# A perceiver layer on one core: the last unit's down products and scatter in column halves, three gathers ahead of a low part on GpSimd

## The chip, the cores and the metric

The kernel runs on one core of one Trainium2 chip. The metric is the time of one execution in microseconds, measured on the device. Smaller is better. The core has five engines with instruction streams of their own: TensorE (PE in the profile; PEld is its loading of stationary operands), VectorE (DVE), ScalarE (ACT), GpSimd (POOL) and SyncE (SP), and sixteen DMA engines that they share. Engines wait for each other through semaphores.

## The reference

One layer of a perceiver: a cross attention of 512 tokens over 8192 context rows, a causal self attention, and a feed-forward part of experts. Everything is float32. The change lies in the last part:

```python
x_flat = x.reshape(Bx * Tx, H)                      # 512 x 512
scores = jax.nn.softmax(x_flat @ gate_w.T, axis=-1)
_, topk_ids = jax.lax.top_k(scores, 2)              # 2 of 8 experts for a token
w = scores * in_topk
gu = jnp.einsum('nh,eih->nei', x_flat, experts_gate_up)
g, u = (gu[..., :704], gu[..., 704:])
h = jax.nn.silu(g) * u
expert_out = jnp.einsum('nei,ehi->neh', h, experts_down)
out = jnp.einsum('neh,ne->nh', expert_out, w)
out = out + shared_weight * shared                  # an expert that sees all tokens
return x + out
```

## The kernel before

**Splitting.** Each float32 operand of a product is split in two: a high part (a rounded copy, made by ScalarE) and a low part (the rest, made by VectorE or GpSimd as `raw - high`). A product is the sum of three: high x high, high x low, low x high. Names end in `_hi` and `_lo`.

**Units.** After the shared expert, the kernel goes through units. A unit is one expert and up to 128 of the token rows routed to it. Each of the eight experts has one unit; experts with more rows have a further one. With these inputs three are added, so units 0 to 10 run, and `final` is 10. The rows of all units lie in a DRAM tensor, `slots`, 128 rows per unit; a unit's result goes back to the place its rows came from. A unit has three hidden chunks (`CH`), of 256, 256 and 192 columns. `up(u, c)` computes both sides of a chunk (12 matmuls), `turn_hidden(u, c)` transposes the product of silu and side, and `down(u, c)` adds the chunk's part to the unit's 128x512 output in bank 2 of PSUM (6, 6 and 5 matmuls).

**The order on TensorE** is written by hand in `unit` (lines 1314 to 1342). The third down part of a unit is done inside the next one: `up(u, 0)`, `down(u - 1, 2)`, `up(u, 1)` and so on. `down(u, 2)` waits for `dn_last_ready >= u + 1`, that is, for the low part of the unit's third down weights, `wd_lo[2]`. For units 0 to 9 GpSimd makes it (`down_last_low`, line 533, waiting for the high part and for the first low part of the next unit's sides); for unit 10 VectorE does. SyncE's load of the next unit's third down part into `raw_d[2]` waits for the same semaphore (line 375).

**What happens to a unit's output.** Units 0 to 8: ScalarE copies it to `y_out` (`keep`), SyncE stores it to `slots` (line 392), nine stores, each adding 16 to `y_stored`. Units 9 and 10 are not stored. Their output is weighed and split (`output_high` on ScalarE, `output_low` on VectorE), and TensorE adds it to the token order by a product with `back`, a 0/1 matrix: `scatter(0)` for unit 9, `scatter(1)` for unit 10, each four token tiles of high and four of low part, into banks 4 to 7. All other tokens' results are gathered: GpSimd issues eight indirect DMAs (`gather_kept`, line 538), four token tiles for each of the two experts of a token (`c`), from `slots` to `met`. Ahead of them stands a wait for all nine stores and an add of one column (line 547). Three semaphores tell of them: `met_full` (four of c=0), `met_second` (c=1, tiles 0 and 1), `met_rest` (c=1, tiles 2 and 3).

**The tail.** VectorE adds six of the eight gathered tiles to `x` with their weight (`add_met`, line 1907). For c=1, tiles 2 and 3, ScalarE multiplies by the weight (line 860) and GpSimd adds (line 554). At last VectorE adds the four banks of the scatter (line 1988), the fourth in two column halves, and each of these adds releases a store: 256 KB for the first three tiles, 128 KB for each half of the fourth, from SyncE (lines 422, 424) and ScalarE (862, 864). Between the last down product and `scatter(1)` TensorE runs warming matmuls (`keep_warm`, line 901).

```python
pool.wait_ge(y_stored, (final - 1) * 16)
pool.tensor_tensor(blank[:, 0:1], blank[:, 0:1], blank[:, 1:2], ALU.add)
gather_kept(0, 0, ST, met_full)
gather_kept(1, 0, 2, met_second)
gather_kept(1, 2, ST, met_rest)
```

## Time and profile before

| | us |
|---|---|
| median of 3 runs | 697.93 (696.33 to 698.01) |
| the profiled execution | 697.82 |
| its span, first to last instruction | 696.1 |
| TensorE busy | 687.5 (99%) |
| VectorE busy | 554.6 (80%) |
| ScalarE busy | 339.2 (49%) |
| GpSimd busy | 211.2 (30%) |
| mean granted clock of TensorE | 0.998 |

The span is the time from the first to the last instruction that the profiler recorded in one execution; the execution's own time is 1.7 us longer. Busy times are sums over the span: they say that TensorE hardly rests, and not which engine is late in the last 30 us, where the change lies. A row of a timeline gives the start, the duration, the engine, the source line, the operation and its tiles; in brackets the idle time before it and what ended it. Matmuls are pipelined: a row's duration is its way through the engine, and the distance of two starts is what it costs. The releaser is inferred from semaphore events.

### The profile page before, as it was taken

The numbers are of one execution on the slowest core, as the hardware profiler recorded it, in microseconds if no ns is written. First come the engines' busy times: TensorE is split into PE (matmuls) and PEld (weight loads), VectorE is DVE, ScalarE is ACT, GpSimd is POOL, SyncE is SP. The second block draws the span as 40 slices with busy tenths as digits, with TensorE's granted clock in tenths as the row PEclk, the third lists the DMA queues.
The fourth block names the chain that finished last, engine by engine and source line by source line (L and its number), as shares of the span: only waits on it lengthen the run. The fifth ranks groups of instructions, "written<-read, shape, count | busy, mean of one in ns | idle before, by whom it ended". The sixth has DMA issues, their size and how long they took to land.

```text
span 696.1 us, 9883 instructions
## 1 busy us (share of the span) xinstructions
PE 687.5 (99%) x3195; PEld 568.7 (82%) x3195; DVE 554.6 (80%) x730; ACT 339.2 (49%) x454; POOL 211.2 (30%) x156
## 2 busy tenths in 40 slices
PE   8999999999999999999999999999999999999997
PEld 7788888888888788888888888888888888878875
DVE  5688877777989998899996853779435799999997
ACT  4422222222245565556663334642234588888872
POOL 5954545545430000000000001236884111211245
PEclk9999999999999999999999999999999999999999
DMA  8057677777742236432210602514200899999984
GB/s 305 15 171 220 214 226 238 245 219 239 246 139 92 91 121 282 152 110 90 90 60 0 252 37 81 234 72 144 91 1 6 312 345 386 370 392 374 378 320 151
DMA packets 38974, 130.70 MB, mean 188 GB/s; under 512 B 6690, under 2 KB 10788, under 8 KB 35876
## 3 DMA queue, kind: packets, MB, share of 16 engines
q1 hardware_dynamic: 36548, 124.72, 50.8%
q0 software_dynamic: 1536, 4.20, 1.9%
q10 hardware_dynamic: 864, 1.44, 0.6%
q8 instruction: 14, 0.23, 0.1%
q14 instruction: 12, 0.10, 0.1%
HBM read 120.89 MB, written 9.46 MB: 187 GB/s over the span
## 4 chain that ended last, share of the span: by engine, by line
PE 80%; DVE 6%; DMA 6%; issue 3%; ACT 3%; SPq 1%; DVEq 0%
PE ps L1065 25%; PE ps L1005 8%; PE ps L1006 8%; PE ps L1009 8%; DMA raw_u<-up_in 5%; PE ps L891 4%; PE ps L893 4%; PE ps L892 4%; PE ps L1258 4%; ACT wu_hi L749 2%; DVE wu_lo L1849 2%; PE ps L958 2%; DVE wd_lo L1855 2%; PE ps L1192 1%; DMA wk<-wk_in 1%
## 5 line engine op out<-in xcount | busy, mean ns | idle before, releaser
L468 POOL TENSOR_TENSOR c_lo<-ring,c_hi 128x512 fp32r<-128x512 f32 x64 | 87.7, 1371 | 86.4 <-ACT c_hi L615 86.4
L615 ACT ACTIVATE c_hi<-ring 128x512 fp32r<-128x512 f32 x64 | 40.4, 634 | 126.4 <-PE ps L1009 82.9
L485 POOL TENSOR_TENSOR w_lo<-raw,w_hi 128x1024 fp32r<-128x1024 f32 x11 | 26.5, 2408 | 247.4 <-ACT w_hi L736 234.6
L1005 PE MATMUL ps<-qk_hi,c_hi 128*128 128x512 f32 x256 | 99.8, 390 | 0.0
L1006 PE MATMUL ps<-qk_lo,c_hi 128*128 128x512 f32 x256 | 99.6, 389 | 0.0
L1494 DVE TENSOR_TENSOR runmax<-runmax,att 128x512 f32<-128x512 f32 x64 | 83.9, 1311 | 3.9
L1488 DVE SCALAR_TENSOR_TENSOR att<-ring,beta,ps 128x512 f32 (+1 forms) x64 | 47.7, 746 | 26.6 <-PE ps L1009 25.7
L1009 PE MATMUL ps<-qk_hi,c_lo 128*128 128x512 f32 x256 | 68.6, 389 | 0.0
L1065 PE MATMUL ps<-p_hi,d_hi 128*128 128x512 f32 x256 | 63.8, 391 | 0.0
L1065 PE MATMUL ps<-p_hi,d_lo 128*128 128x512 f32 x256 | 63.2, 389 | 0.0
L1065 PE MATMUL ps<-p_lo,d_hi 128*128 128x512 f32 x256 | 63.2, 389 | 0.0
L749 ACT ACTIVATE wu_hi<-raw_u 128x2048 fp32r<-128x2048 f32 (+1 forms) x33 | 58.7, 1778 | 6.0 <-DMA raw_u<-up_in 5.8
L1849 DVE TENSOR_TENSOR wu_lo<-raw_u,wu_hi 128x1024 fp32r<-128x1024 f32 x40 | 51.8, 1294 | 11.4 <-ACT wu_hi L749 11.1
L533 POOL TENSOR_TENSOR wd_lo<-raw_d,wd_hi 128x1024 fp32r<-128x1024 f32 x10 | 24.1, 2413 | 117.7 <-DVE wu_lo L1849 117.7
L639 ACT ACTIVATE d_hi<-ring 128x1024 fp32r<-128x1024 f32 x32 | 33.9, 1059 | 50.0 <-PE ps L1065 49.3
L1005 PEld LDWEIGHTS ps<-qk_hi,c_hi 128*128 128x128 f32 x256 | 48.0, 188 | 10.5 <-DVE qk_lo L1468 0.6
L1065 PEld LDWEIGHTS ps<-p_lo,d_hi 128*128 128x128 f32 x256 | 48.1, 188 | 10.0
L1065 PEld LDWEIGHTS ps<-p_hi,d_lo 128*128 128x128 f32 x256 | 48.1, 188 | 10.0
L1009 PEld LDWEIGHTS ps<-qk_hi,c_lo 128*128 128x128 f32 x256 | 48.0, 188 | 10.0
L1065 PEld LDWEIGHTS ps<-p_hi,d_hi 128*128 128x128 f32 x256 | 47.6, 188 | 10.5 <-DVE ps L1590 0.8
L1006 PEld LDWEIGHTS ps<-qk_lo,c_hi 128*128 128x128 f32 x256 | 48.1, 188 | 9.9
L1267 PE MATMUL ps<-wu_hi,xg_hi 128*128 128x512 f32 (+1 forms) x132 | 50.9, 386 | 0.0
(340 smaller groups left out, 1507.1 us busy)
## 6 DMA issues: line engine op xcount, KB each, us to landing
ring<-stream SPq DMA_DIRECT2D x64, 512.0 KB, 4.3
raw_u<-up_in SPq DMA_DIRECT2D x22, 1024.0 KB, 7.0
raw_d<-down_in SPq DMA_DIRECT2D x33, 512.0 KB, 7.9
ring<-ctx_in SPq DMA_DIRECT2D x32, 512.0 KB, 3.3
raw<-shared_in SPq DMA_DIRECT2D x11, 768.0 KB, 6.1
raw_u<-up_last_in SPq DMA_DIRECT2D x11, 768.0 KB, 7.5
slots<-blank SPq DMA_DIRECT2D x15, 256.0 KB
late<-wqkv_in SPq DMA_DIRECT2D x1, 3072.0 KB, 10.3
```

Source lines behind the costliest of these rows:

```text
L468: pool.tensor_tensor(c_lo[:, s % 2, :], ring1[:, s, 0, :], c_hi[:, s % 2, :].bitcast(F32), ALU.subtract).then_inc(lo1_ready, 1)
L615: act.activation(c_hi[:, s % 2, :], ring1[:, s, 0, :], ACT.Copy).then_inc(hi1_ready, 1)
L639: act.activation(d_hi[s % 2][:, :, :], ring2[:, s, :, :], ACT.Copy).then_inc(hi2_ready, 1)
L749: act.activation(wu_hi[c][:, :, :], raw_u[c][:, :, :], ACT.Copy).then_inc(up_hi_ready, 1)
L1005: pe.matmul(ps[:, s, :], hi, qk_hi[:, k, :], start=(k == 0), stop=False)
L1006: pe.matmul(ps[:, s, :], hi, qk_lo[:, k, :], start=False, stop=False)
L1009: return pe.matmul(ps[:, s, :], c_lo[:, s % 2, k * P:(k + 1) * P], qk_hi[:, k, :], start=False, stop=(k == KC - 1))
L1065: mm = pe.matmul(ps[:, 4 + d, :], a[s % 2][:, t, d * P:(d + 1) * P], b[s % 2][:, t, :], start=(opening and t == 0), stop=False, skip_group ...
L1267: pe.matmul(out_, xg_hi[:, k, :], wu_hi[c][:, k, :], start=(k == 0), stop=False)
L1488: dve.scalar_tensor_tensor(out=att[:, g * U + s, :], in0=ring1[:, s, 1, :], scalar=beta[:, 0:1], in1=ps[:, s, :], op0=ALU.mult, op1=ALU.ad ...
L1494: dve.tensor_tensor(runmax[:, :], runmax[:, :], att[:, g * U + s, :], ALU.max).then_inc(max_done, 1)
L1849: ins = dve.tensor_tensor(wu_lo[c][:, k, :], raw_u[c][:, k, :], wu_hi[c][:, k, :].bitcast(F32), ALU.subtract)
```

## The change

- **GpSimd**: the loop of low parts ends one unit earlier. The wait for the nine stores and the column add follow, then the first three gathers, then the low part of unit 9, then the other five gathers. At the end GpSimd adds the right column half of token tile 3, which ScalarE copied from PSUM for it.
- **TensorE**: in the last unit all down products are computed in two column halves of 256, the left in bank 2, the right in bank 1; each half of the third part adds to `y_psum_e` by itself. The warming matmuls before the last scatter are gone. The last scatter takes the high rows by halves and then, by token tile, the low rows of both halves.
- **ScalarE**: weighs the gathered tiles 2 and 3 (`weigh_rest`, with the wait for `met_rest`) before the last unit's rows and no longer after them; makes the high rows in two halves; then copies the right half of bank 7 to `met[:, 0, 0, right]` and issues the store of the right half after GpSimd's add.
- **VectorE**: makes the low rows in two halves, and adds only the left half of tile 3, for which it now also waits for ScalarE's copy.

```diff
@@ -39,3 +39,2 @@
 WARM = 8
-WARM_END = 4
 WARM3 = (4, 3)
@@ -235,2 +234,4 @@
         ps = scope.enter_context(nc.psum_tensor("ps", [P, 8, 512], F32))
+
+        y_parts = ((slice(0, D // 2), ps[:, 2, 0:D // 2]), (slice(D // 2, D), ps[:, 1, 0:D // 2]))
 
@@ -296,2 +297,4 @@
 
+        left, right = slice(0, D // 2), slice(D // 2, D)
+
         block = scope.enter_context(nc.Block())
@@ -422,4 +425,4 @@
                 sp.dma_start(out[st * P:(st + 1) * P, :], x[:, st, :]).then_inc(out_stored, 16)
-            sp.wait_ge(added, 2 * ST + 2 + 5)
-            sp.dma_start(out[3 * P:S, D // 2:D], x[:, 3, D // 2:D]).then_inc(out_stored, 16)
+            sp.wait_ge(added, 2 * ST + 2 + 4)
+            sp.dma_start(out[3 * P:S, left], x[:, 3, left]).then_inc(out_stored, 16)
             sp.wait_ge(out_stored, 16 * (ST + 1))
@@ -543,3 +546,3 @@
             final = pool.value_load(more[0:1, 0:1], min_val=0, max_val=MORE) + (E - 1)
-            with pool.Fori(1, final) as e:
+            with pool.Fori(1, final - 1) as e:
                 down_last_low(e)
@@ -547,3 +550,5 @@
             pool.tensor_tensor(blank[:, 0:1], blank[:, 0:1], blank[:, 1:2], ALU.add)
-            gather_kept(0, 0, ST, met_full)
+            gather_kept(0, 0, ST - 1, met_full)
+            down_last_low(final - 1)
+            gather_kept(0, ST - 1, ST, met_full)
             gather_kept(1, 0, 2, met_second)
@@ -554,2 +559,5 @@
                 pool.tensor_tensor(x[:, st, :], x[:, st, :], met[:, 1, st, :], ALU.add).then_inc(met_added, 1)
+            pool.wait_ge(met_step, 3)
+            pool.wait_ge(met_added, 2)
+            pool.tensor_tensor(x[:, 3, right], x[:, 3, right], met[:, 0, 0, right], ALU.add).then_inc(met_added, 1)
 
@@ -768,7 +776,18 @@
 
-            def output_high(u, n):
-
+            def output_high(u):
                 act.wait_ge(y_psum_e, u * CH + CH)
-                act.wait_ge(info_read, n + 1)
+                act.wait_ge(info_read, 1)
                 act.activation(y_hi[:, :], ps[:, 2, :], ACT.Copy, scale=info_s[:, 1:2]).then_inc(y_hi_ready, 1)
+
+            def last_output_high(u):
+                act.wait_ge(info_read, 2)
+                for h, (part, from_) in enumerate(y_parts):
+                    act.wait_ge(y_psum_e, u * CH + (CH + h))
+                    act.activation(y_hi[:, part], from_, ACT.Copy, scale=info_s[:, 1:2]).then_inc(y_hi_ready, 1)
+
+            def weigh_rest():
+                act.wait_ge(met_rest, 16 * (ST - 2))
+                for st in range(ST // 2, ST):
+                    act.activation(met[:, 1, st, :], met[:, 1, st, :], ACT.Copy,
+                                   scale=weight_of[:, 1, st:st + 1]).then_inc(met_step, 1)
 
@@ -804,3 +823,4 @@
                     hidden_high(u, 2, last)
-                    output_high(u, 1)
+                    weigh_rest()
+                    last_output_high(u)
 
@@ -857,9 +877,8 @@
             unit(final, last=True)
-            act.wait_ge(met_rest, 16 * (ST - 2))
-            for st in range(ST // 2, ST):
-                act.activation(met[:, 1, st, :], met[:, 1, st, :], ACT.Copy, scale=weight_of[:, 1, st:st + 1]).then_inc(met_step, 1)
+            act.wait_ge(out_psum, ST)
+            act.activation(met[:, 0, 0, right], ps[:, 4 + ST - 1, right], ACT.Copy).then_inc(met_step, 1)
             act.wait_ge(added, 2 * ST + 2 + 2)
             act.dma_start(out[P:2 * P, :], x[:, 1, :]).then_inc(out_stored, 16)
-            act.wait_ge(added, 2 * ST + 2 + 4)
-            act.dma_start(out[3 * P:S, 0:D // 2], x[:, 3, 0:D // 2]).then_inc(out_stored, 16)
+            act.wait_ge(met_added, 3)
+            act.dma_start(out[3 * P:S, right], x[:, 3, right]).then_inc(out_stored, 16)
 
@@ -1278,3 +1297,3 @@
 
-            def down(u, c):
+            def down(u, c, last=False):
                 pe.wait_ge(hl_ready, u * CH + (c + 1))
@@ -1284,10 +1303,13 @@
                     pe.wait_ge(dn_last_ready, u + 1)
-                for t in range(2 if c < 2 else 1):
-                    hi, lo = (h[:, c, t * P:(t + 1) * P] for h in (hh_e, hl_e))
-                    for i, (a, b) in enumerate(((hi, wd_hi), (hi, wd_lo), (lo, wd_hi))):
-                        mm = pe.matmul(ps[:, 2, :], a, b[c][:, t, :], start=(c == 0 and t == 0 and i == 0), stop=False)
-                if c == 2:
-                    pe.matmul(ps[:, 2, :], hh_e[:, 2, P:2 * P], wd_hi[2][:, 1, :], start=False, stop=False)
-                    mm = pe.matmul(ps[:, 2, :], hh_e[:, 2, P:2 * P], wd_lo[2][:, 1, :], start=False, stop=True)
-                mm.then_inc(y_psum_e, 1)
+                for part, out_ in y_parts if last else ((slice(0, D), ps[:, 2, :]),):
+                    for t in range(2 if c < 2 else 1):
+                        hi, lo = (h[:, c, t * P:(t + 1) * P] for h in (hh_e, hl_e))
+                        for i, (a, b) in enumerate(((hi, wd_hi), (hi, wd_lo), (lo, wd_hi))):
+                            mm = pe.matmul(out_, a, b[c][:, t, part], start=(c == 0 and t == 0 and i == 0), stop=False)
+                    if c == 2:
+                        pe.matmul(out_, hh_e[:, 2, P:2 * P], wd_hi[2][:, 1, part], start=False, stop=False)
+                        mm = pe.matmul(out_, hh_e[:, 2, P:2 * P], wd_lo[2][:, 1, part], start=False, stop=True)
+                        mm.then_inc(y_psum_e, 1)
+                if c < 2:
+                    mm.then_inc(y_psum_e, 1)
 
@@ -1299,15 +1321,26 @@
 
-            def scatter(n):
-
-                pe.wait_ge(back_ready, n + 1)
+            def to_tokens(st, values, part, **flags):
+                return pe.matmul(ps[:, 4 + st, part], back[:, st * P:(st + 1) * P], values[:, part],
+                                 skip_group_check=True, **flags)
+
+            def scatter_before():
+                pe.wait_ge(back_ready, 1)
                 for part, ready in ((y_hi, y_hi_ready), (y_lo, y_lo_ready)):
-                    pe.wait_ge(ready, n + 1)
+                    pe.wait_ge(ready, 1)
                     for st in range(ST):
-                        mm = pe.matmul(ps[:, 4 + st, :], back[:, st * P:(st + 1) * P], part[:, :],
-                                       start=(n == 0 and part is y_hi), stop=(n == 1 and part is y_lo),
-                                       skip_group_check=True)
-                        if n == 1 and part is y_lo:
-                            mm.then_inc(out_psum, 1)
-                if n == 0:
-                    mm.then_inc(scattered, 1)
+                        mm = to_tokens(st, part, slice(0, D), start=(part is y_hi), stop=False)
+                mm.then_inc(scattered, 1)
+
+            def scatter_last():
+                pe.wait_ge(back_ready, 2)
+                for h in range(2):
+                    pe.wait_ge(y_hi_ready, 2 + h)
+                    for st in range(ST):
+                        to_tokens(st, y_hi, y_parts[h][0], start=False, stop=False)
+                for st in range(ST):
+                    for h in range(2):
+                        if st == 0:
+                            pe.wait_ge(y_lo_ready, 2 + h)
+                        mm = to_tokens(st, y_lo, y_parts[h][0], start=False, stop=(h == 1))
+                    mm.then_inc(out_psum, 1)
 
@@ -1326,3 +1359,3 @@
                 if last:
-                    scatter(0)
+                    scatter_before()
                 up(u, 2)
@@ -1333,3 +1366,3 @@
                     pe.wait_ge(y_ready, u)
-                down(u, 0)
+                down(u, 0, last)
                 if last:
@@ -1337,7 +1370,6 @@
                 turn_hidden(u, 2, last)
-                down(u, 1)
+                down(u, 1, last)
                 if last:
-                    down(u, 2)
-                    keep_warm(WARM_END, 1)
-                    scatter(1)
+                    down(u, 2, last)
+                    scatter_last()
 
@@ -1893,6 +1925,5 @@
 
-            def output_low(n):
-
-                dve.wait_ge(y_hi_ready, n + 1)
-                dve.scalar_tensor_tensor(out=y_lo[:, :], in0=ps[:, 2, :], scalar=info_s[:, 1:2], in1=y_hi[:, :].bitcast(F32),
+            def output_low(ready, part, from_):
+                dve.wait_ge(y_hi_ready, ready)
+                dve.scalar_tensor_tensor(out=y_lo[:, part], in0=from_, scalar=info_s[:, 1:2], in1=y_hi[:, part].bitcast(F32),
                                          op0=ALU.mult, op1=ALU.subtract).then_inc(y_lo_ready, 1)
@@ -1919,3 +1950,3 @@
                 if last:
-                    output_low(0)
+                    output_low(1, slice(0, D), ps[:, 2, :])
                 down_low(u, 1)
@@ -1950,3 +1981,4 @@
                     add_met(1, 0, 2)
-                    output_low(1)
+                    for h in range(2):
+                        output_low(2 + h, *y_parts[h])
 
@@ -1986,4 +2018,6 @@
                     dve.wait_ge(met_added, st - 1)
-                for part in (slice(0, D),) if st < 3 else (slice(0, D // 2), slice(D // 2, D)):
-                    dve.tensor_tensor(x[:, st, part], x[:, st, part], ps[:, 4 + st, part], ALU.add).then_inc(added, 1)
+                if st == ST - 1:
+                    dve.wait_ge(met_step, 3)
+                part = slice(0, D) if st < ST - 1 else left
+                dve.tensor_tensor(x[:, st, part], x[:, st, part], ps[:, 4 + st, part], ALU.add).then_inc(added, 1)
 
```

On GpSimd's queue at the end of the loop over units (`wd_lo_176` is the low part of the third down weights, `blank` the column add, `met<-slots` a gather) it was:

```order
L533 TENSOR_TENSOR wd_lo_176<-raw_d_164,wd_hi_173 128x1024 [waits up_lo_ready]
L544 ISA
L544 COMPARE_AND_BRANCH
L546 ISA
L547 TENSOR_TENSOR blank<-blank 128x1 [waits y_stored]
L538 DMA met<-slots,kept_of 128x512 x8
L554 TENSOR_TENSOR x<-x,met 128x512 [waits met_step,added]
L554 TENSOR_TENSOR x<-x,met 128x512 [waits met_step]
```

and is now:

```order
L550 TENSOR_TENSOR blank<-blank 128x1 [waits y_stored]
L541 DMA met<-slots,kept_of 128x512 x3
L534 ISA
L535 REGISTER_ALU [waits dn_hi_ready]
L536 TENSOR_TENSOR wd_lo_176<-raw_d_164,wd_hi_173 128x1024 [waits up_lo_ready]
L541 DMA met<-slots,kept_of 128x512 x5
L559 TENSOR_TENSOR x<-x,met 128x512 [waits met_step,added]
L559 TENSOR_TENSOR x<-x,met 128x512 [waits met_step]
L562 TENSOR_TENSOR x<-x,met 128x256 [waits met_added,met_step]
```

The low part of unit 9 (the row at line 536; the row at line 533 above stands in the loop) now has the wait for the stores, the column add and three gathers in front of it, and a third add has come at the end.

On ScalarE after the last unit's transposed hidden chunks (`hh_e`) it was:

```order
L761 ACTIVATE hh_e<-ps 128x256 [waits hT_psum] x2
L773 ACTIVATE y_hi<-ps,info_s 128x512 [waits info_read,y_psum_e]
L860 ACTIVATE met<-met,weight_of 128x512 [waits met_rest]
L860 ACTIVATE met<-met,weight_of 128x512
L862 DMA result<-x 128x512 [waits added]
L864 DMA result<-x 128x256 [waits added]
```

and is now:

```order
L769 ACTIVATE hh_e<-ps 128x256 [waits hT_psum] x2
L791 ACTIVATE met<-met,weight_of 128x512 [waits met_rest]
L791 ACTIVATE met<-met,weight_of 128x512
L786 ACTIVATE y_hi<-ps,info_s 128x256 [waits y_psum_e,info_read]
L785 REGISTER_ALU
L786 ACTIVATE y_hi<-ps,info_s 128x256 [waits y_psum_e]
L879 ACTIVATE met<-ps 128x256 [waits out_psum]
L881 DMA result<-x 128x512 [waits added]
L883 DMA result<-x 128x256 [waits met_added]
```

The wait for the last gathers (`met_rest`) has moved ahead of the rows, the rows are two, and a copy from PSUM stands before the stores.

## Rows read from the trace of the kernel before

**Rows 1.** The page's first part: busy time, share of the span, instructions.

```profile
PE 687.5 (99%) x3195; PEld 568.7 (82%) x3195; DVE 554.6 (80%) x730; ACT 339.2 (49%) x454; POOL 211.2 (30%) x156
```

**Rows 2.** The chain that ended last: start, duration, what.

```profile
692.77 0.42 DVE x L1988
```

**Rows 3.** Timeline of TensorE, from unit 9's third down part on.

```profile
675.33 0.39 PE L1288 MATMUL ps<-wd_hi,hh_e 128*128 128x512 f32 x1
...
679.52 0.44 PE L1275 MATMUL ps<-ident,hid_e 128*128 128x128 f32 x2 [0.17 <-DVE hid_e L1872]
...
687.01 0.50 PE L1288 MATMUL ps<-wd_hi,hh_e 128*128 128x512 f32 x1
...
690.30 1.08 PE L1306 MATMUL ps<-y_lo,back 128*128 128x512 f32 x4
```

**Rows 4.** Timeline of GpSimd, from 656 us to the end.

```profile
670.36 2.41 POOL L533 TENSOR_TENSOR wd_lo<-raw_d,wd_hi 128x1024 fp32r<-128x1024 f32 x1 [11.20 <-DVE wu_lo L1849]
672.71 1.19 POOL L547 TENSOR_TENSOR blank<-blank 128x1 f32<-128x1 f32 x1
674.05 1.00 POOL L538 DMA_INDIRECT met<-slots,kept_of  x1 [0.15 <-issue]
...
678.40 1.43 POOL L538 DMA_INDIRECT met<-slots,kept_of  x1 [0.30 <-issue]
...
685.50 1.09 POOL L538 DMA_INDIRECT met<-slots,kept_of  x1 [0.31 <-issue]
690.14 2.53 POOL L554 TENSOR_TENSOR x<-x,met 128x512 f32<-128x512 f32 x2 [3.54 <-ACT met L860]
```

**Rows 5.** Timeline of SyncE's queue, the last store of rows and the last of the result.

```profile
664.22 0.43 SPq L392 DMA_DIRECT2D slots<-y_out  x1
...
693.55 0.33 SPq L424 DMA_DIRECT2D result<-x  x1
```

**Rows 6.** DMAs: the store at 664.22, nine such stores, third-part loads, last gather; us to landing.

```profile
slots<-y_out SPq DMA_DIRECT2D x1, 256.0 KB, 8.0
...
DMA to landing us min/median/max: 5.7/7.7/8.0
...
DMA to landing us min/median/max: 8.1/8.3/8.5
...
met<-slots,kept_of POOLq DMA_INDIRECT x1, 3.7
```

**Rows 7.** Timeline of VectorE.

```profile
672.06 1.79 DVE L1849 TENSOR_TENSOR wu_lo<-raw_u,wu_hi 128x1024 fp32r<-128x1024 f32 x1 [0.45 <-ACT wu_hi L749]
...
677.79 1.22 DVE L1855 TENSOR_TENSOR wd_lo<-raw_d,wd_hi 128x1024 fp32r<-128x1024 f32 x1
...
687.59 1.41 DVE L1907 SCALAR_TENSOR_TENSOR x<-met,weight_of,x 128x512 f32<-128x512 f32 x2
```

**Rows 8.** Stretches of time, TensorE: length, busy (instructions), granted clock, DMA share, GB/s.

```profile
693.20:693.40 0.20, 0.00 (x0) 1.00 1.00 358
...
693.60:693.80 0.20, 0.00 (x0) 0.50 1.01 379
```

**Rows 9.** TensorE at the start: its timeline, and one line's durations in ns (min/median/max).

```profile
2.06 3.78 PE L901 MATMUL ps<-ident,ones 128*128 128x128 f32 x16 [2.06 <-POOLq L442]
...
L907 PE MATMUL ps<-wk_hi,wq_hi x16: 387/389/796, 5.6 to 19.0; 128*128 128x512 f32 x16
```

**Rows 10.** Timeline of TensorE, two neighbouring matmuls of 256 columns.

```profile
455.59 0.28 PE L1192 MATMUL ps<-l_hi,w_lo 128*128 128x256 f32 x1
455.71 0.28 PE L1192 MATMUL ps<-l_hi,w_hi 128*128 128x256 f32 x1
```

**Rows 11.** Timeline of ScalarE in the last unit.

```profile
680.27 1.05 ACT L753 ACTIVATE wd_hi<-raw_d 128x1024 fp32r<-128x1024 f32 x1
...
685.77 0.38 ACT L761 ACTIVATE hh_e<-ps 128x256 fp32r<-128x256 f32 x1 [1.23 <-PE ps L1275]
688.47 0.69 ACT L773 ACTIVATE y_hi<-ps,info_s 128x512 fp32r<-128x512 f32 x1 [2.31 <-PE ps L1291]
```

More of the change, by code:

```diff
@@ L783, in unit @@
                 if last:
-                    output_high(u - 1, 0)
+                    output_high(u - 1)
                 elif not first:
```

## The prediction

> **What bounds the kernel now.** The engine summary comes first: TensorE is busy 687.5 of 696.1 us [rows 1], so any hole in its stream goes into the time almost whole. The change touches only the last unit and the unit before it, so I read next the chain of waits there. Its last link is VectorE's add at 692.77 [rows 2]; ahead of it stand VectorE's other adds and TensorE's products and scatter, back to 679.52. There TensorE had waited 0.17 us for VectorE's product [rows 3]: that is all the slack it has after 675.
>
> TensorE's timeline [rows 3] shows the place that matters most: at 675.33 it starts the third down product of the next-to-last unit (unit 9 of 0 to 10), which needs `wd_lo[2]`, GpSimd's low part. GpSimd's timeline [rows 4] shows that low part at 670.36, 2.41 us long, done at 672.77, 2.56 us early. Behind it stand the wait for the stored rows (`y_stored`) with the one-column add, and eight gathers, from 674.05 to 686.6. The store that this wait is for was issued at 664.22 [rows 5] and took 8.0 us to land, so 672.2; the nine stores of this kind took 5.7 to 8.0 us, with a median of 7.7 [rows 6].
>
> **Three gathers ahead of the low part.** The order on GpSimd is now: wait for the store, add, three gathers, low part, five gathers. GpSimd looks idle for 11.2 us before its low part [rows 4], but the wait for the store is no part of that idle time: nothing behind it can begin before 672.2. From there:
> - The one-column add. It took 1.19 us before, though its work is one column. The VectorE operation beside it, a difference that read two tiles from SBUF, ran from 672.06 to 673.85, with 1.79 us where the same shape takes 1.22 at 677.79 [rows 7]: the two engines hold each other up. In the new order that difference should end by 673.3, and I let the add end there (bounds: 0.1 us after the landing, to 673.9 as now).
> - Three gathers: from the first's start to the fourth's were 4.35 us, 0.30 of it the pause before the fourth, so 4.05 [rows 4], and 0.15 ahead of the first: 677.5 (bounds: at 1.00 us each, the fastest, with two pauses, 3.6; and as now).
> - The low part, 2.41: done at 679.96 (bounds 678.5 and, if it must first let a VectorE operation of 1.22 us end, 681.7).
>
> TensorE is ready at 675.33 and now starts at about 680.0: **+4.65 us**, less the 0.17 of idle that this covers, so +4.5 (bounds 3.0 to 6.2). Nothing hides it: TensorE issues in order, and what follows (the second side, 12 matmuls) stands behind that wait. VectorE's cover goes too: its chain up to 679 is 4.5 us ahead afterwards and then waits for TensorE.
>
> On the shared access of the two engines the Trainium skill (SBUF — State Buffer, Who interferes with whom) says that a VectorE instruction with two SBUF inputs and a GpSimd instruction that reads SBUF exclude each other for the whole instruction, whoever comes first. The 1.79 against 1.22 agrees. By it the low part, ready at 677.5, would be shut out by the difference that runs at 677.79 [rows 7] if that starts first, and end near 681, a microsecond later than in my sum.
>
> **The clock after the hole.** This is a cost that the diff doesn't name. After the last matmul, which ends near 691.4, the granted clock stays at 1.00 for two microseconds and is at 0.50, the 1.2 GHz level, from 693.6 [rows 8]; up to the end it is 1.00, the 2.4 GHz level. A hole of 4.65 us is longer than those 2.2 us. What work costs at the low level the start of the program shows: the first 128x512 matmuls took up to 796 ns against 389, and from 2.06 to about 7 us everything ran at half pace [rows 9] (the clock column says 1.00 there; the durations are the better witness). So 5 us of work took the low level before it rose, of which half, 2.5 us, was lost. Bounds 0 and 2.6; I take 1.9, nearer to the start, because there too the engine came from rest, and less since part of that stretch was small transposes. The Trainium skill (TensorE: Matmul & The Clock Gate, Part 1: The HAM clock gate) states that an idle array falls to 1.2 GHz and that sustained work brings 2.4 back; the trace agrees at both ends of the program. By that rule the hole would not come without its slow stretch; the sum without the rule would be 701.5.
>
> **What is behind the low part on other queues.** SyncE's load of the last unit's third down part waits for that low part, too: issued at 680.0 instead of 672.97. It needs to be in SBUF when ScalarE comes to it, which was at 680.27 [rows 11] and is now about 685; the two loads of this size before it took 8.1 and 8.5 us in the full queue [rows 6], but now it is alone with gathers. Cost 0; if it takes all of 8, ScalarE's next silu is a microsecond late. The eighth gather was issued at 685.50 and landed 3.7 later [rows 4, 6]; now it is issued 6 to 7.3 us after the low part, so lands at 689.7 to 691.
>
> **The down products in halves.** 17 matmuls of 512 columns become 34 of 256, and the eight of the scatter 16. Matmuls of 256 columns started 0.12 us apart [rows 10], those of 512 0.23 [rows 3]: each pair costs 0.01 us more, +0.17 for the down products; some of it lies beside VectorE's wait at 687.0, so +0.1. In return the first half is complete 0.6 us before the second, and ScalarE's first row half runs beside the second.
>
> **The tail, by the times of before.** ScalarE's two row halves (0.69 for a whole; 0.35 to 0.69 for a half, I take 0.48) end at 688.4 and 689.0 instead of 689.16 [rows 11]. VectorE is busy with its adds until 688.99 [rows 7], so the low halves end at 689.5 and 689.9, where the whole ended at 689.94: little is won there. The high scatter ends at 689.6 instead of 690.2, the low one starts its second half at 690.0, and the four token tiles are ready from 690.26 to 690.98; before, 690.7 to 691.4. So 0.4. The weighing of tiles 2 and 3 (2 x 0.7 on ScalarE) goes ahead of the rows, so GpSimd's two adds, which ended at 692.67 just before VectorE's fourth at 692.77 [rows 2, 4], are out of the way. VectorE's list of adds loses its last half: 0.33. It gains a wait: its last add now needs ScalarE's copy of the right half (0.38, done at 691.4), before its turn at 692.2, so 0. GpSimd's half add (0.64 to 1.27, I take 0.7) ends at 692.2, and its store goes out at 692.25. The last store goes out at 692.65 instead of 693.55 [rows 5]: **-0.9** (bounds -0.3 and -1.3). Removing the warming matmuls costs 0: they fill a pause of 0.9 us.
>
> The weighing has a price of its own: it waits for the eighth gather, and the rows stand behind it on ScalarE. ScalarE came free at 686.15 [rows 11], and that gather landed at 689.2. Were nothing else moved, ScalarE would weigh until 690.6 and the rows would come 2 us late. Here TensorE's delay covers it: ScalarE comes free at 686.15+4.5+1.9=692.5, after the landing.
>
> **Sum.** +4.5 +1.9 +0.1 -0.9 = +5.6. The profiled execution took 697.82 (span 696.1), 0.11 under the median of 697.93. Forecast: 697.8+5.6 = **703.4 us**.
>
> **Rivals.**
> - The hole, but the clock stays (chance 0.17): +3.7, so 701.5. For it: in the end the clock held for two microseconds of rest, and the phase of its fall need not repeat. Against: the hole is twice as long.
> - No hole, faster or equal (0.07): the store lands early enough that three gathers and the low part are over by 675.33. It would have to land by 675.33-2.41-4.05-0.25=668.6, 4.4 us after its issue; against it, the shortest of nine took 5.7. Then only the tail counts: 697.8-0.8 = 697.0, provided the gathers start as early as that. This is the one on the other side.
> - A longer hole (0.15): the low part is shut out by VectorE, or the third down load takes 8 us, or the eighth gather is late: +1 to +2 on the forecast, 704.4 to 705.6.
> - The forecast itself: 0.61.
>
> **Range and chances.** The bounds of the hole and of the clock without rare cases give +2.5 to +7.8: 700.3 to 705.6. Below it lie the case of no hole and a few of the short ones, above it the worst of the third. A difference of 0.3% (2.1 us) is what a measurement of this kernel can tell from no change; slower by more than that means above 700.0: 0.87. The shortest hole at the clock's high level and the case without one (697.0 lies within 2.1 of 697.93) give 0.11 for the same; 0.02 is left for faster, should the tail give twice what I count.
>
> **What would show it.** In the changed profile: GpSimd's one-column add right after 672.2, three gathers, then `wd_lo` ending near 680; TensorE idle 4 to 5 us before its third down product, with GpSimd's low part as releaser; granted clock below 1.00 in the slice behind it, and 128x512 matmuls 0.43 us apart there; from the second down part on the same distances as before; the last store 5.6 us after the last down matmul instead of 6.5. I am wrong if TensorE's wait is under 2 us, or if the matmuls behind it start 0.23 apart from the first one on.

## The result, and the profile after

| | before | changed |
|---|---|---|
| median, us | 697.72 (696.33 to 698.01, 4 runs) | 705.30 (704.33 to 707.03, 4 runs) |
| the profiled execution | 697.82 | 704.33 |
| its span | 696.1 | 702.6 |
| last store issued at | 693.55 [rows 5] | 699.58 |
| mean granted clock of TensorE | 0.998 | 0.994 |

The ratio is 1.012, with a 95% interval of 1.0104 to 1.0136: **slower, by 7.6 us in the medians and 6.5 in the profiled executions**. The forecast was +5.6 (703.4 us). The quotient of the two medians is 1.0109, inside the interval; the interval reaches from 7.3 to 9.5 us, so the tenths of the 7.6 say little. The profiled execution of the changed kernel is the quickest of its four; the other three had spans of 703.0, 704.1 and 705.3 us, with mean clocks of 0.990 and 0.991.

The page says little, as before [rows 1]: TensorE works 1.8 us more, and the span is 6.5 longer, so some 4.7 us of rest have come in.

```profile
PE 689.3 (98%) x3212; PEld 571.0 (81%) x3212; DVE 565.2 (80%) x730; ACT 339.6 (48%) x456; POOL 207.2 (29%) x157
```

GpSimd's timeline, where [rows 4] had the low part at 670.36:

```profile
671.37 0.20 POOL L550 TENSOR_TENSOR blank<-blank 128x1 f32<-128x1 f32 x1 [12.55 <-DMA slots<-y_out]
671.71 1.00 POOL L541 DMA_INDIRECT met<-slots,kept_of  x1
...
675.57 3.03 POOL L536 TENSOR_TENSOR wd_lo<-raw_d,wd_hi 128x1024 fp32r<-128x1024 f32 x1
...
691.71 2.51 POOL L559 TENSOR_TENSOR x<-x,met 128x512 f32<-128x512 f32 x2 [6.79 <-ACT met L791]
698.78 0.73 POOL L562 TENSOR_TENSOR x<-x,met 128x256 f32<-128x256 f32 x1 [4.56 <-ACT met L879]
```

The store landed at 671.4, three gathers took to 675.57, and the low part ended at 678.60. TensorE's timeline, the rows that answer to [rows 3], with those of the slow stretch and of the end:

```profile
674.78 0.39 PE L1288 MATMUL ps<-wu_hi,xg_lo 128*128 128x512 f32 x1
678.75 0.47 PE L1308 MATMUL ps<-wd_hi,hh_e 128*128 128x512 f32 x1 [3.58 <-POOL wd_lo L536]
...
680.22 0.63 PE L1287 MATMUL ps<-wu_lo,xg_hi 128*128 128x512 f32 x1
680.64 0.63 PE L1288 MATMUL ps<-wu_hi,xg_lo 128*128 128x512 f32 x1
...
691.80 0.35 PE L1308 MATMUL ps<-wd_hi,hh_e 128*128 128x256 f32 x1
...
692.95 0.28 PE L1311 MATMUL ps<-wd_lo,hh_e 128*128 128x256 f32 x1
694.56 1.22 PE L1323 MATMUL ps<-y_hi,back 128*128 128x256 f32 x8 [1.33 <-DVE back L1924]
696.40 1.89 PE L1323 MATMUL ps<-y_lo,back 128*128 128x256 f32 x8 [0.62 <-DVE y_lo L1928]
```

Three things are to be seen. The third down product waits 3.58 us for GpSimd. Behind it, from 680.22 on, neighbours start 0.42 to 0.43 us apart instead of 0.23. And at the end, where TensorE went from the last down product to the scatter with only its warming matmuls between, it now waits 1.33 us for `back` (the 0/1 matrix), a VectorE result that before was there in time, and then 0.62 us for `y_lo`. The first of these waits costs little, since the warming matmuls filled most of that time before: the high scatter starts 1.61 us after the last down matmul (692.95 to 694.56) instead of 1.26 (688.04 to 689.30). The low one starts 3.45 us after it instead of 2.26. Stretches of the changed trace (length, busy and instructions of PE, PEld, DVE, ACT, POOL, then granted clock, DMA share, GB/s) show the clock of the second:

```profile
679.00:680.00 1.00, 1.00 (x6) 0.78 (x6) 1.00 (x2) 0.00 (x0) 0.72 (x1) 1.00 0.48 33
680.00:681.00 1.00, 1.00 (x4) 0.83 (x3) 0.87 (x3) 0.69 (x1) 0.98 (x1) 0.60 0.32 131
...
682.00:683.00 1.00, 1.00 (x4) 0.81 (x3) 0.78 (x1) 0.00 (x0) 0.69 (x2) 0.50 1.00 369
...
684.00:685.00 1.00, 1.00 (x7) 0.79 (x6) 0.06 (x1) 0.48 (x2) 0.92 (x1) 1.00 0.58 184
```

Eight matmuls ran at the 1.2 GHz level, each 0.20 us dearer: 1.6 us. (The clock fell once more behind the two waits of the end: from 697.3 it is at 0.50, and the eight low scatter matmuls took 1.89 us instead of the 1.45 of the kernels below in which it stayed at 1.00. VectorE's last adds run back to back from 697.28 all the same, so this moved the last store by little.) VectorE's timeline shows why `back` was late:

```profile
674.65 1.75 DVE L1873 TENSOR_TENSOR wu_lo<-raw_u,wu_hi 128x1536 fp32r<-128x1536 f32 x1
676.32 2.31 DVE L1898 COPY info_s<-info_all 128x2 f32 x1
...
691.74 1.27 DVE L1898 COPY info_s<-info_all 128x2 f32 x1
693.05 1.45 DVE L1924 TENSOR_SCALAR back<-token_row,info_s 128x512 fp32r<-128x512 f32 x1
694.42 1.40 DVE L1938 SCALAR_TENSOR_TENSOR x<-met,weight_of,x 128x512 f32<-128x512 f32 x2
695.86 0.88 DVE L1928 SCALAR_TENSOR_TENSOR y_lo<-ps,info_s,y_hi 128x256 fp32r<-128x256 f32 x2
...
697.28 2.21 DVE L2022 TENSOR_TENSOR x<-x,ps 128x512 f32<-128x512 f32 x4 [0.55 <-PE ps L1323]
```

A copy of two columns takes 2.31 us beside GpSimd's low part and 1.27 beside its first add (691.71); `back` takes 1.45 beside the second and ends when both are over. The two adds of gathered tiles behind it keep their own duration (1.40), but they and `y_lo`, which stands behind them in VectorE's order, start nearly two microseconds late against the last down matmul, and that is what the low scatter waits for. In the kernel before, GpSimd's adds stood at 690.14 [rows 4], 2.1 us behind the start of the last down matmul and behind both instructions; now they start 1.2 us ahead of it. They came forward because ScalarE now weighs ahead of the rows:

```profile
690.85 1.32 ACT L791 ACTIVATE met<-met,weight_of 128x512 f32<-128x512 f32 x2
693.05 0.84 ACT L786 ACTIVATE y_hi<-ps,info_s 128x256 fp32r<-128x256 f32 x2 [0.88 <-DVE info_s L1898]
```

**The balance**, from three distances between rows of the two profiled executions. The start of unit 9's third down part moved from 675.33 to 678.75, +3.4. From there to the start of the last unit's third down part it was 11.68 us (675.33 to 687.01) and is 13.05 (678.75 to 691.80), +1.4: clock and halves, less waits that were covered. From there to the last store it was 6.54 and is 7.78, **+1.2**. The sum is +6.0, and the last store's landing (2.6 us instead of 2.1) brings the span to +6.5.

### The profile page after: what moved, and what is told of

It is laid out like the page before. It is cut to its first block, busy times and chain, and to the rows that moved or that the text cites. A ratio compares the mean times of both kernels' runs of the same rounds, so it can differ in the third digit from the quotient of the medians.

```text
span 702.6 us, 9920 instructions
## 1 busy us (share of the span) xinstructions
PE 689.3 (98%) x3212; PEld 571.0 (81%) x3212; DVE 565.2 (80%) x730; ACT 339.6 (48%) x456; POOL 207.2 (29%) x157
## 4 chain that ended last, share of the span: by engine, by line
PE 86%; issue 5%; DVE 3%; DMA 2%; ACT 2%; POOL 1%; POOLq 0%; DVEq 0%; SPq 0%
PE ps L1084 25%; PE ps L1024 8%; PE ps L1028 8%; PE ps L1025 8%; PE ps L910 4%; PE ps L911 4%; PE ps L912 4%; PE ps L1277 4%; PE ps L1308 2%; DMA raw_u<-up_in 2%; PE ps L1288 2%; PE ps L1287 2%; PE ps L1286 2%; PE ps L926 2%; PE ps L977 2%
## 5 line engine op out<-in xcount | busy, mean ns | idle before, releaser
L471 POOL TENSOR_TENSOR c_lo<-ring,c_hi 128x512 fp32r<-128x512 f32 x64 | 84.8, 1325 | 89.5 <-ACT c_hi L623 89.5
L1526 DVE TENSOR_TENSOR runmax<-runmax,att 128x512 f32<-128x512 f32 x64 | 92.9, 1452 | 3.9
```

Of the source, the lines that this page charges most:

```text
L471: pool.tensor_tensor(c_lo[:, s % 2, :], ring1[:, s, 0, :], c_hi[:, s % 2, :].bitcast(F32), ALU.subtract).then_inc(lo1_ready, 1)
L1526: dve.tensor_tensor(runmax[:, :], runmax[:, :], att[:, g * U + s, :], ALU.max).then_inc(max_done, 1)
```

## The experiments

Their times stand beside runs of the kernel before on the same chip: median 696.82 for the first four, 696.84 for the next four, 697.02 for the last. The theory after reading the trace: hole and slow clock as forecast, and a tail that lost 1.2 us because GpSimd's adds, moved forward by the weighing, held VectorE up. The rivals: the tail lost its time to the halves or to the weighing's place on ScalarE; the slow matmuls have another cause than the rest.

**GpSimd's order alone**, in the kernel before:

```
-            with pool.Fori(1, final) as e:
+            with pool.Fori(1, final - 1) as e:
...
-            gather_kept(0, 0, ST, met_full)
+            gather_kept(0, 0, ST - 1, met_full)
+            down_last_low(final - 1)
+            gather_kept(0, ST - 1, ST, met_full)
```

> The kernel before with GpSimd's new order alone: wait for the nine stores, column add, three gathers, low part of unit 9, five gathers. Theory A (the whole change is a hole, a slow stretch of the clock behind it and a tail in which GpSimd's two adds shut VectorE out): the hole of 3.6 to 3.8 us stays, the granted clock falls to 0.50 for about 3.5 us behind it (1.6 us), and the tail is that of before, 5.1 us from the last down matmul to the issue of the last store; span 696.1+3.6+1.6 = 701.3, time about 703.0, some 2.3 us under the changed kernel. Rival B (the loss in the tail comes from the column halves or from late gathers, not from the place of the weighing): same value here, so this run only sizes the order. Rival C (the new order costs little by itself): under 699.

Measured: 703.60 us (703.11 to 704.53), ratio 1.0098 (1.0085 to 1.0111), so +6.8 us. The order is most of the loss, and the tail is no part of it: from the last down matmul to the last store it is 5.3 us (693.33 to 698.66), against 5.5 before. Rows of VectorE, GpSimd and TensorE of this kernel:

```profile
676.50 3.77 DVE L1857 TENSOR_TENSOR wd_lo<-raw_d,wd_hi 128x1024 fp32r<-128x1024 f32 x1
...
676.82 2.36 POOL L533 TENSOR_TENSOR wd_lo<-raw_d,wd_hi 128x1024 fp32r<-128x1024 f32 x1
...
679.32 0.49 PE L1290 MATMUL ps<-wd_hi,hh_e 128*128 128x512 f32 x1 [4.90 <-POOL wd_lo L533]
```

Here GpSimd's low part ran at its own pace and VectorE's difference, 1.22 us by itself [rows 7], lasted until 1.1 us after the low part's end; in the changed kernel VectorE's 1.75-us difference came first and the low part took 3.03. Which of the two instructions pays differs between these two executions.

**The rest of the change alone** (the changed kernel, with GpSimd's gathers behind the last low part again):

```
-            with pool.Fori(1, final - 1) as e:
+            with pool.Fori(1, final) as e:
...
-            gather_kept(0, 0, ST - 1, met_full)
-            down_last_low(final - 1)
-            gather_kept(0, ST - 1, ST, met_full)
+            gather_kept(0, 0, ST, met_full)
```

> The changed kernel with GpSimd's order of before: no gather ahead of the low part, all else as changed. Theory A: no hole over 0.3 us, clock 1.00 up to the end. ScalarE's weighing waits for the eighth gather, about 689.2, so the rows come 1.5 to 2 us late, and GpSimd's adds run beside VectorE's last adds; last store issued 1 to 2.5 us later than before; time 699 to 700.5. Rival B (the halves are worth 0.9 us and the weighing ahead of them costs nothing): 697.0.

Measured: 699.97 us (698.38 to 700.67), ratio 1.0041 (1.0028 to 1.0055): +2.9 us by the ratio, 3.15 by the medians. Rows of ScalarE and TensorE of this kernel:

```profile
688.39 1.33 ACT L789 ACTIVATE met<-met,weight_of 128x512 f32<-128x512 f32 x2 [3.37 <-DMA met<-slots,kept_of]
689.63 0.82 ACT L784 ACTIVATE y_hi<-ps,info_s 128x256 fp32r<-128x256 f32 x2
...
690.23 2.05 PE L1321 MATMUL ps<-y_hi,back 128*128 128x256 f32 x8 [2.92 <-ACT y_hi L784]
```

As the prediction said of the weighing: with no delay of TensorE to cover it, ScalarE waits 3.37 us for the eighth gather, and rows and scatter behind it wait too. TensorE's pause has a price of its own here: the granted clock falls to 0.50 at 689.5 and stays there, and the eight high scatter matmuls take 2.05 us where they took 1.18 at the high level (in the same kernel with the weighing late, below). So "the tail" is no gain of its own; without the hole it is a loss by another way.

**The weighing behind the row halves**, the rest as changed:

```
-                    weigh_rest()
                     last_output_high(u)
+                    weigh_rest()
```

> The changed kernel with the weighing of the gathered tiles 2 and 3 moved back behind ScalarE's two row halves. Theory A: the copy of the slot numbers and the making of the scatter matrix on VectorE take 0.17 and 0.49 us again instead of 1.27 and 1.45, since GpSimd's two adds come later; the last store is issued 4.3 to 4.9 us after the last down matmul instead of 6.3; time 1.5 to 2 us under the changed kernel, 703.5. Hole and slow clock unchanged. Rival D (VectorE was slow there because the low part and the gathers had delayed it, or because of the DMA traffic): both operations stay over 1 us and the time stays at 705.3.

Measured: 702.95 us (701.36 to 704.07), ratio 1.0082 (1.0066 to 1.0097), against 1.0120 (1.0104 to 1.0136) of the whole change: 0.38%, 2.6 us less. Rows of VectorE:

```profile
693.25 0.17 DVE L1898 COPY info_s<-info_all 128x2 f32 x1
693.46 0.49 DVE L1924 TENSOR_SCALAR back<-token_row,info_s 128x512 fp32r<-128x512 f32 x1
```

Copy and `back` have their own durations again, GpSimd's adds start at 696.00, and from the start of the last down matmul (694.45) to the last store (699.42) it is 5.0 us instead of 6.6 (692.95 to 699.58). That is 1.6 us by the profile. Its span (702.0) is only 0.6 shorter, because in this one execution the rest was longer (4.55 us) and twelve matmuls behind it, not eight, ran at the low level; the medians, over six and four runs, are the better measure. So the weighing's place on ScalarE turned the tail's gain into a loss. With the weighing late the gain is there, 5.0 us against the 5.5 of the kernel before, and the warming matmuls are gone here too, so neither the halves nor their absence made the loss.

**A warm hole**: the changed kernel with 16 small matmuls, which nothing reads and which the trace shows as 32 rows of 128 columns, ahead of the third down product, in the hole.

```
                 up(u, 0)
+                if last:
+                    keep_warm(16, 1)
                 if not first:
                     down(u - 1, 2)
```

> The changed kernel with 16 warming matmuls on TensorE ahead of unit 9's third down part, in the hole (bank 1, which is free there). Theory A: they end before the low part does, so the third down product starts when it did, but the granted clock stays 1.00, the eight matmuls at 0.43 us are 0.23 apart, and the span is 1.6 us shorter than the changed kernel's; and its runs lie closer together than 704.3 to 707.0, because that spread is the length of the slow stretch. Rival E (the slow stretch is absorbed by other waits): no gain, or a loss.

Measured: 703.02 us (702.63 to 703.55), ratio 1.0089 (1.0076 to 1.0102). Rows of TensorE, then of VectorE:

```profile
673.70 3.73 PE L920 MATMUL ps<-ident,ones 128*128 128x128 f32 x32
678.81 0.47 PE L1308 MATMUL ps<-wd_hi,hh_e 128*128 128x512 f32 x1 [1.38 <-POOL wd_lo L536]
679.12 0.40 PE L1308 MATMUL ps<-wd_lo,hh_e 128*128 128x512 f32 x1
...
690.37 1.40 DVE L1926 TENSOR_SCALAR back<-token_row,info_s 128x512 fp32r<-128x512 f32 x1
691.69 2.44 DVE L1940 SCALAR_TENSOR_TENSOR x<-met,weight_of,x 128x512 f32<-128x512 f32 x2
```

The product starts as late as before (678.81), but from 679.12 on the matmuls start 0.23 us apart, and the span is 1.7 us shorter (700.9). The slow stretch was the price of the rest, not of the data or of the DMA traffic. Its runs lie within 0.9 us of each other, those of the changed kernel within 2.7. That the clock made that spread is not shown: of the changed kernel's four runs the one with the lowest mean clock (0.990) is the second quickest, and the wait-ahead kernel below, without a slow stretch, spreads over 3.3 us. The tail's loss is still there: `back` is held again, and the two adds take 2.44 instead of 1.41 [rows 7].

**The wait and the column add ahead of the low part, no gather**, in the kernel before: is it the wait or the gathers?

```
             pool.wait_ge(y_stored, (final - 1) * 16)
             pool.tensor_tensor(blank[:, 0:1], blank[:, 0:1], blank[:, 1:2], ALU.add)
+            down_last_low(final - 1)
             gather_kept(0, 0, ST, met_full)
```

(The loop ahead of it ends one unit earlier, as above.)

> The kernel before, but with the wait for the nine stores and the column add ahead of unit 9's low part and all eight gathers behind it: no gather ahead. Theory A (the hole is the landing of the last store, plus the gathers ahead, plus the low part, less the time at which TensorE gets there): the low part starts near 671.8 and ends near 674.3, before TensorE needs it at 674.5 to 675, so no hole, clock 1.00, and the time of before within 0.3 us. Rival F (the wait for the stores by itself makes the hole): TensorE idle over 1 us and the time at least 1.5 us up.

Measured: 699.55 us (698.58 to 701.87), ratio 1.0045 (1.0030 to 1.0060). A miss: there was no hole (TensorE waited 0.34 us for the low part), yet it cost 2.7 us. Rows of VectorE and TensorE:

```profile
672.40 2.96 DVE L1850 TENSOR_TENSOR wu_lo<-raw_u,wu_hi 128x1024 fp32r<-128x1024 f32 x1
...
684.74 1.41 DVE L1908 SCALAR_TENSOR_TENSOR x<-met,weight_of,x 128x512 f32<-128x512 f32 x2 [1.93 <-DMA met<-slots,kept_of]
...
686.94 0.44 PE L1276 MATMUL ps<-ident,hid_e 128*128 128x128 f32 x2 [1.68 <-DVE hl_e L1882]
```

The low part, at 671.87, stood beside VectorE's difference, which took 2.96 us instead of 1.23, and TensorE lost 0.74 at 679.27 to that chain. The fourth gather was issued at 679.89 instead of 678.40, so VectorE stood 1.93 us at its first adds of gathered tiles, which wait for all four, with the `hl` that TensorE needs queued behind them: 1.68. A low part 1.5 us later is not free, even where TensorE hardly waits for it.

**Six gathers ahead**, in the kernel before (`gather_kept(0, 0, ST, met_full)` and `gather_kept(1, 0, 2, met_second)` stand ahead of `down_last_low(final - 1)`):

> The kernel before with the new order and six gathers ahead of the low part instead of three. Theory A: three more gathers at 1.25 to 1.4 us each make the hole 3.8 to 4.3 us longer than with three (where TensorE stood 4.9 us): about 9 us. The slow stretch of the clock comes once, as before, so it adds little (0 to 1 us); time 707 to 708.5. Rival G (VectorE shuts GpSimd out, and that sets the hole, not the gathers): VectorE has run dry by then, so the hole grows by under 3 us.

Measured: 708.15 us (706.39 to 708.56), ratio 1.0154 (1.0138 to 1.0169), +11.3. A row of TensorE:

```profile
683.22 0.76 PE L1289 MATMUL ps<-wd_hi,hh_e 128*128 128x512 f32 x1 [8.82 <-POOL wd_lo L533]
```

Three gathers more, 3.9 us more of hole, 4.5 us more of time than the same order with three: each gather ahead goes into the time whole. Eleven matmuls ran at the low level behind a rest of 8.8 us, not many more than the eight behind 4.9; the three more are 0.6 us, which is the difference of 3.9 and 4.5.

**The rest of the change, with the weighing behind the rows** and GpSimd's order of before (both edits above together):

> The changed kernel without its two harmful parts: GpSimd's order of before, and the weighing behind the row halves. Left are the column halves and GpSimd's half add. Theory A: no hole, no slow clock, rows not late; last store 0.3 to 0.7 us earlier than before after the last down matmul; time 0.3 to 0.6 under the kernel before, near what a measurement can tell. GpSimd's half add stands behind its two whole adds, so it may take back half of that. Rival B (the halves cost as much as they give): the time of before or 0.5 over it.

Measured: 697.06 us (695.83 to 698.02, 11 runs), ratio 1.0001 (0.9992 to 1.0010). Rows of ScalarE and VectorE:

```profile
687.90 1.34 ACT L789 ACTIVATE met<-met,weight_of 128x512 f32<-128x512 f32 x2 [0.55 <-DMA met<-slots,kept_of]
...
691.36 0.42 DVE L2020 TENSOR_TENSOR x<-x,ps 128x256 f32<-128x256 f32 x1 [0.52 <-POOL x L557]
```

The expected 0.3 to 0.6 us did not come. The scatter is complete earlier, but the weighing waits for the eighth gather, GpSimd's adds wait for the weighing, and VectorE's last add waits for them. The last store is issued 5.6 us after the start of the last down matmul (686.56 to 692.16), as before. Against the same kernel with the weighing ahead of the rows (699.97) it is 2.9 us faster.

**The column halves alone**, without GpSimd's half add and ScalarE's copy for it (VectorE makes both halves of the last add again, as in the kernel before), the warming matmuls gone. From the edit:

```
-                part = slice(0, D) if st < ST - 1 else left
-                dve.tensor_tensor(x[:, st, part], x[:, st, part], ps[:, 4 + st, part], ALU.add).then_inc(added, 1)
+                for part in (slice(0, D),) if st < 3 else (left, right):
+                    dve.tensor_tensor(x[:, st, part], x[:, st, part], ps[:, 4 + st, part], ALU.add).then_inc(added, 1)
```

(The weighing and GpSimd's order stand as before.)

> The kernel before with only the column halves of the last unit's down products, rows and scatter (no warming matmuls); order, weighing and all adds as before. Theory A: the low scatter ends 0.4 us earlier, VectorE's adds follow, the last store goes out 0.3 to 0.5 us earlier; time 0.3 to 0.5 under the kernel before. Against the run with GpSimd's half add this tells what that add gives: by theory A nothing, within 0.3 us.

Measured: 697.10 us (695.75 to 698.71, 11 runs), ratio 1.0004 (0.9995 to 1.0013): nothing. A row of VectorE:

```profile
692.40 0.75 DVE L2013 TENSOR_TENSOR x<-x,ps 128x256 f32<-128x256 f32 x2 [0.54 <-POOL x L557]
```

The same wait, at the same place. ScalarE's weighing, which GpSimd's adds need, waited 0.65 us for the eighth gather (688.93): the end hangs on that.

**Two more adds on GpSimd**, behind its last gather, in the kernel before, where GpSimd has nothing to do: the exclusion by itself.

```
             gather_kept(1, 2, ST, met_rest)
+            for _ in range(2):
+                step(pool.tensor_tensor(y_out[:, :], token_row[:, :], token_row[:, :], ALU.add))
```

> The kernel before, with two more GpSimd additions (128x512 each, of a row tile to itself, into a tile that nothing reads) right behind its last gather, about 686.6 to 689.2 us; the output stays that of the reference. Theory A (GpSimd's additions shut VectorE out, whatever VectorE's instruction reads): some of VectorE's copy of info (0.17 us before), its back (0.49), its add of the weighed rows or its add of the scattered rows, those that fall beside the two additions, measure over 1 us instead of their own time, and the last store is issued 1 to 2.5 us later, at 694.5 to 696 on this profile's clock: 698 to 699.5 us. Rival D (VectorE is not held up, the tail of the changed kernel lost its time to the order of the weighing alone): the same instructions keep 0.17 and 0.49 us, and the time is that of before within 0.5 us, since GpSimd is idle there.

Measured: 698.39 us (697.50 to 699.27, 8 runs), ratio 1.0020 (1.0009 to 1.0031). GpSimd's and VectorE's timelines of this kernel:

```profile
685.44 2.17 POOL L552 TENSOR_TENSOR y_out<-token_row 128x512 f32<-128x512 f32 x2
688.89 2.71 POOL L556 TENSOR_TENSOR x<-x,met 128x512 f32<-128x512 f32 x2 [1.28 <-ACT met L862]
...
685.82 0.72 DVE L1868 COPY info_s<-info_all 128x2 f32 x1
686.57 1.33 DVE L1894 TENSOR_SCALAR back<-token_row,info_s 128x512 fp32r<-128x512 f32 x1
...
689.25 0.75 DVE L1899 SCALAR_TENSOR_TENSOR y_lo<-ps,info_s,y_hi 128x512 fp32r<-128x512 f32 x1
```

The copy ends when the first add does, `back` when the second does: 0.72 and 1.33 instead of 0.17 and 0.48. The low scatter waits 0.77 us for `y_lo`. From the start of the last down matmul to the last store it is 6.4 us (686.87 to 693.24) instead of 5.5, and the whole costs 1.4 us. Two of the numbers expected were missed: the copy stayed under 1 us, and the last store went out before 694.5, since in this execution the last down matmul lay 1.2 us earlier than in that of before; distance and time fit. The rival, that GpSimd's adds hold nothing up, is out. So is the DMA traffic as the cause in the changed kernel: the DMA engines' share is 0.00 there from 691.5 to 694.5. And `y_lo`, which reads PSUM, took its usual 0.75 beside the adds.

## Why the prediction was wrong, point by point

The direction was right, and so were the hole and the slow clock behind it, which are most of the loss; the size was two microseconds short, and the tail had the wrong sign. That the sum came this close is in part luck: hole, clock and halves together came out 1.7 us under their terms (4.8 instead of 6.5), the tail 2.1 over its own, and the last store's landing 0.5 longer, which no term had.

- **The hole, forecast +4.5** (third down product from 675.33 to 680.0): it started at 678.75, +3.4 (the rest before it is 3.58 in the profile). The store landed at 671.4 and not at 672.2, the column add took 0.20 and the gathers 3.86 instead of 4.05. The low part took 3.03 and not 2.41, since a VectorE difference had begun first. Within the bounds of 3.0 to 6.2. That the gathers and not the wait make the hole, the wait-ahead and six-gather kernels show. The same order gave a start at 679.32, 679.34 and 678.81 in three other kernels, so this term differs by 0.6 us between executions.
- **The clock, +1.9**: eight matmuls at half pace, 1.6, in the profiled execution. The warm hole takes 1.7 away: shown. The Trainium skill (TensorE: Matmul & The Clock Gate, Part 1: The HAM clock gate) states that an idle array falls to the low level; the trace agrees, here in the middle of the program. What I left out is that the size of this term differs between executions: eight to twelve slow matmuls in the profiles of three kernels with the same order, 0.8 us between the ends. A forecast for the median needs that.
- **Halves, +0.1**: the last unit's third down part took 0.12 us more (1.15 from its first start to its last, 1.03 before); in the time it is too small to be seen, alone they gave 1.0004.
- **The tail, -0.9** ("The tail, by the times of before"; bounds -0.3 and -1.3): **this is the step that failed**. It was +1.2 by the profile: from the last unit's third down part to the last store 7.8 us, where 5.6 was forecast and 6.5 measured before. I took VectorE's and ScalarE's durations from rows of before and wrote that GpSimd's two adds "are out of the way" once the weighing is ahead of the rows. They went out of the way of VectorE's last add and into the way of `info` and `back`: 0.17 and 0.48 us became 1.27 and 1.45, everything behind them on VectorE came nearly two microseconds late, and TensorE, ScalarE and the last store waited (in the warm-hole kernel the adds of the gathered tiles were held too, 2.44 instead of 1.41). I had used the exclusion of the two engines for the low part, as a rival, and had not asked it again of the adds that this change moves; nor had I taken in that it reaches one-input instructions. The weigh-late kernel (own durations back, tail 1.6 us shorter) and the two adds show it. What was left of the forecast gain is small: with the weighing late the same distance is 6.1 us (693.30 to 699.42), -0.4 instead of -0.9, and without the hole the time is that of before.
- **The price of the weighing itself**: rightly foreseen as hidden by TensorE's delay, and as about 2 us without it; the rest of the change alone lost 2.9, and 2.9 came back when the weighing went behind the rows.
- **"Removing the warming matmuls costs 0"**: the pause that they filled had grown, and the low scatter fell to the low level (1.89 instead of 1.45 us). The last store hardly moved by it, and where the pause stayed short (weighing late, halves alone) the clock stayed at 1.00.
- **The third down load and the eighth gather**: neither was late; ScalarE weighed at 690.85 without a wait.
- A slip in the rivals: +1 to +2 on the forecast is 704.4 to 705.4, not 705.6.

By its parts: GpSimd's order alone +0.98%, the rest alone +0.41%, together 1.39% against 1.20% measured; the rest alone contains the wait for the eighth gather, which the hole hides.

Open: why the slow stretch differs from one execution to the next, and how the 1.1 us between the profiled +6.5 and the median +7.6 is divided between the hole's end, the slow stretch and the rest; only one execution of each kernel was profiled. No version tried beats the kernel before. Those that end level are held by the eighth gather; one that brings it forward without putting gathers ahead of the low part was not tried.

## What to carry to other kernels

When an edit moves work on GpSimd, list what VectorE does in the new time of each moved instruction, and let each of those that read only SBUF end when GpSimd's ends, not after its own duration. Then follow what stands behind them in VectorE's order. Work put ahead of the operand of the engine that never rests goes into the time whole once the operand's lead is used up, and a rest of several microseconds had a slow stretch of TensorE behind it. And splitting the last stage gained nothing here while its end hung on a transfer: follow the last add back to its latest input first.

## What the runs showed of the hardware that was not expected

- GpSimd's elementwise instructions, from SBUF to SBUF, held up VectorE instructions that read one SBUF tile, too: a copy of 128x2 took 0.72 and 1.27 us beside an add of 128x512 and 2.31 beside the low part of 128x1024, instead of 0.17; a TENSOR_SCALAR of 128x512 took 1.33 to 1.45 instead of 0.48. `y_lo`, which reads one operand from PSUM, was not held (0.75 beside GpSimd's adds). The section of the Trainium skill that the prediction draws on (SBUF — State Buffer, Who interferes with whom) states more than the prediction took from it: `copy` and `tensor_scalar` can enter modes that take the shared ports, where their operands allow it. The traces agree.
- The difference that lost in the GpSimd-order kernel was recorded as begun 0.3 us ahead of the low part (676.50 and 676.82), and still ended 1.1 us behind it (680.27 and 679.18): the recorded start did not tell which of the two went first.
- After 3.6 us of rest the clock column of the changed kernel shows 1.00 for the first microsecond of work and the low level only then; in the GpSimd-order kernel, after 4.9 us, the second matmul already had 0.61 us.
- How long the low level lasts did not go by the length of the rest: eight matmuls after 3.6 and 4.9 us, twelve after 4.6, eleven after 8.8.
- Shorter waits brought the low level as well, and late: in the changed kernel TensorE waited 1.33 and 0.62 us at the end with eight matmuls between, and the clock fell 0.9 us after the second wait was over (697.3).
